# Softmax normalisation split between VectorE and GpSimd, and k rotated on GpSimd without a break

## The reference, cut to what matters

```
q = rope(layernorm(x) @ wq.T)      16 heads of 64
k = rope(ctx @ wk.T)
v = ctx @ wv.T
scores = where((j <= i) & (j >= i - 64), q.k / 8, -1e30)
probs  = softmax(scores)           <- exp, row sum, multiply by 1/sum
x = x + tanh(g0) * ((probs @ v) @ wo.T)
x = x + tanh(g1) * ffn(layernorm(x))   2 shared experts, 16 routed experts, top 4, exact gelu
```

## Time and profile before

| | |
|---|---|
| median of the runs | 564.47 us |
| profiled execution | 565.92 us, span 564.1 us |
| TensorE busy | 524.5 us, 93% |
| VectorE busy | 323.0 us, 57% |
| ScalarE busy | 308.1 us, 55% |
| GpSimd busy | 278.9 us, 49%, nearly all of it before 330 us |
| granted TensorE clock, mean | 0.985 |
| GpSimd divides (L415) | 64, 1040 ns each |
| GpSimd turns (L402) and joins (L410) | 29 of each, 2409 and 2377 ns |

### The profile page before, as it was taken

The page is one execution under the profiler, slowest core; times in us unless marked ns, Lnnn a source line. Parts: engine busy times, 40 slices in busy tenths (PEclk is TensorE's granted clock), DMA queues, the critical chain, the costliest instruction groups (busy, mean ns, idle before and its releaser), DMA issues.

```text
span 564.1 us, 13070 instructions
## 1 busy us (share of the span) xinstructions
PE 524.5 (93%) x4914; PEld 460.8 (82%) x4914; DVE 323.0 (57%) x1043; ACT 308.1 (55%) x864; POOL 278.9 (49%) x203
## 2 busy tenths in 40 slices
PE   8869799999999999999889789889989998999997
PEld 5557788888888888988778679779978997889996
DVE  2965567456865667666656735463645454554444
ACT  4255686566675656757466745753345334533332
POOL 2798988688787867888678515530010001000000
PEclk9989899999999999999999999999989998999999
DMA  6523312111031101111111155207200540045000
GB/s 238 181 55 95 91 38 90 35 34 34 3 109 34 35 2 34 35 35 43 32 34 52 41 191 203 76 1 232 107 2 0 154 185 1 1 137 202 1 1 37
DMA packets 20173, 41.02 MB, mean 73 GB/s; under 512 B 2896, under 2 KB 3152, under 8 KB 20112
## 3 DMA queue, kind: packets, MB, share of 16 engines
q1 hardware_dynamic: 20112, 40.20, 22.8%
HBM read 30.62 MB, written 2.23 MB: 58 GB/s over the span
## 4 chain that ended last, share of the span: by engine, by line
PE 64%; issue 20%; DVE 7%; POOL 4%; ACT 3%; DMA 1%; POOLq 0%; ACTq 0%
PE ring L807 42%; PE psO L1005 6%; PE psS L974 5%; PE psS L807 5%; PE psT L986 4%; POOL wl L423 1%; DVE arena L642 1%; DVE wl L712 1%; ACT xn L547 1%; POOL rstd L449 1%; DVE arena L645 1%; DMA craw<-in_ctx 1%; PE ring L902 1%; ACT sneg L489 1%; PE psT L947 1%
## 5 line engine op out<-in xcount | busy, mean ns | idle before, releaser
L807 PE MATMUL ring<-xTh,wh 128*128 128x512 f32 x272 | 111.7, 411 | 3.7 <-DVE xTl L613 2.1
L807 PE MATMUL ring<-xTh,wl 128*128 128x512 f32 x272 | 107.3, 394 | 0.0
L807 PE MATMUL ring<-xTl,wh 128*128 128x512 f32 x272 | 107.3, 394 | 0.0
L489 ACT ACTIVATE sneg<-ring 128x512 f32<-128x512 f32 x72 | 43.0, 597 | 103.5 <-PE ring L807 96.4
L691 DVE TENSOR_TENSOR prob<-sneg,arena 128x512 f32<-128x512 f32 x64 | 45.9, 717 | 83.1 <-ACT sneg L489 82.7
L402 POOL TENSOR_TENSOR arena<-arena,sin 128x1024 f32<-128x1024 f32 x29 | 69.9, 2409 | 30.0 <-DVE arena L642 30.0
L807 PE MATMUL ring<-wh,oTh 128*128 128x256 f32 x272 | 78.5, 289 | 3.9 <-DVE oTl L699 2.8
L807 PE MATMUL ring<-wl,oTh 128*128 128x256 f32 x272 | 76.8, 282 | 0.0
L807 PE MATMUL ring<-wh,oTl 128*128 128x256 f32 x272 | 76.7, 282 | 0.0
L415 POOL TENSOR_TENSOR prob<-prob,rinv 128x512 f32<-128x512 f32 x64 | 66.5, 1040 | 20.4 <-DVE rinv L772 19.2
L410 POOL TENSOR_TENSOR arena<-arena 128x1024 f32<-128x1024 f32 x29 | 68.9, 2377 | 1.2
(11 more groups left out here) (118 smaller groups left out, 1194.1 us busy)
## 6 DMA issues: line engine op xcount, KB each, us to landing
arena<-gate_scratch SPq DMA_DIRECT2D x64, 256.0 KB, 6.6
raw<-in_e SPq DMA_DIRECT2D x18, 256.0 KB, 2.6
raw<-in_w SPq DMA_DIRECT2D x16, 256.0 KB, 3.6
arena<-arena SPq DMA_DIRECT2D x16, 256.0 KB, 3.1
arena<-arena SPq DMA_DIRECT2D x16, 192.0 KB, 3.4
craw<-in_ctx SPq DMA_DIRECT2D x4, 512.0 KB, 4.2
x<-in_x SPq DMA_DIRECT2D x4, 512.0 KB, 4.9
out<-x SPq DMA_DIRECT2D x8, 256.0 KB, 2.8
```

What stands on the lines that cost most here:

```text
L489: act.activation(act_g[:, n % 2, :], ring[0][:, n % 2, :], ACT.Gelu).then_inc(f_gelu, 1)
L807: last = pe.matmul(out, a, b, start=start and i == 0 and j == 0, stop=stop and i == n - 1 and j == 2, skip_group_check=check)
```

## The change

VectorE does the multiplication for the even chunks right behind its reciprocal, with a wait on its own instruction between the two. GpSimd does it for the odd chunks alone. The semaphore is split in two, one for each engine, and TensorE and VectorE wait for the one that belongs to the chunk. On GpSimd join(k) moves from step 3 up to step 2, right behind turn(k) and ahead of the divide of that step.

```diff
+        def normed(c):
+            return s_norm[c % 2], c // 2 + 1
...
             def divide(c):
-                pool.wait_ge(s_inv, c + 1)
+                pool.wait_ge(s_inv, c // 2 + 1)
                 pool.tensor_tensor(prob[:, c % BUFS, :, :], prob[:, c % BUFS, :, :],
                                    rinv[:, c % BUFS, :].unsqueeze(2).to_broadcast([P, TT, P]),
-                                   ALU.mult).then_inc(s_norm, 1)
+                                   ALU.mult).then_inc(s_norm[1], 1)
...
                     if k == 2 and u:
                         turn(1, u + 1)
-                    if k == 3 and u:
                         join(1, u + 1)
-                if 1 <= c <= CHUNKS:
+                if 1 <= c <= CHUNKS and c % 2 == 0:
                     divide(c - 1)
...
                 if c >= BUFS:
-                    dve.wait_ge(s_norm, c - BUFS + 1)
-                dve.reciprocal(rinv[:, c % BUFS, :], rsum[:, c % BUFS, :]).then_inc(s_inv, 1)
+                    dve.wait_ge(*normed(c - BUFS))
+                ins = dve.reciprocal(rinv[:, c % BUFS, :], rsum[:, c % BUFS, :])
+                if c % 2:
+                    ins.then_inc(s_inv, 1)
+                else:
+                    link(ins)
+                    dve.tensor_tensor(prob[:, c % BUFS, :, :], prob[:, c % BUFS, :, :],
+                                      rinv[:, c % BUFS, :].unsqueeze(2).to_broadcast([P, TT, P]),
+                                      ALU.mult).then_inc(s_norm[0], 1)
...
             def transpose_probs(c):
-                pe.wait_ge(s_norm, c + 1)
+                pe.wait_ge(*normed(c))
```

More of the change, by code:

```diff
@@ L152, in build @@
         s_pe, s_max, s_exp = sem("s_pe"), sem("s_max"), sem("s_exp")
-        s_inv, s_norm = sem("s_inv"), sem("s_norm")
+        s_inv = sem("s_inv")
+        s_norm = [sem("s_norm_v"), sem("s_norm_p")]
         p_pe, p_out = sem("p_pe"), sem("p_out")
```

## The result

The change makes the kernel **slower by 0.9%**: ratio 1.0087, 95% interval 1.0050 to 1.0124; medians 570.32 us against 567.04 us over 16 runs each. The means are 570.9 and 566.0 us when two long runs of the kernel before (1010.11 and 570.25 us) are left out, and the loss of about 4.9 us is their difference; the medians alone differ by 3.3 us. A second series gave 1.0086 (1.0054 to 1.0117). Forecast was 566.4 us, within 560 to 571, and a loss of 1.9 us. The direction and the class within 2% were right, the size was not.

The account below looks back on a forecast made before the run. TensorE sets the time, bound by the end of GpSimd's join(k) in ten units; +3.2 +2.0 -2.1 -1.2 -1.4 +1.4 = +1.9 us on the profiled 565.92 gives 567.8, less 1.45 for the run median: 566.4 us, range 560 to 571.

Parts of the forecast that it names:

- rival C: VectorE's multiplication is not blocked by GpSimd, one input being a 128x4 tile read repeatedly; -10.0, 554.5 us, chance 0.13.
- Rival B: GpSimd's divide(4u+1) gets in ahead of VectorE's waiting multiplication and ends 0.40 us earlier; -2.1, 562.4 us, chance 0.17.
- a typical unit: Attention unit where join(k) was the bound: divide(4u+1) ends at 122.24, so scores come 0.36 us later than before.
- the nine units: The seven units with 0.69 us of TensorE idle time plus units 12 and 14: 9 x 0.36 = +3.2 us.
- the cover of `oTl`: In a typical unit, `oTl` ends 1.07 us later, at 118.40; the y product wants it at 118.57, leaving 0.17 us.
- Unit 13: LayerNorm statistics on VectorE come 1.07 us later and one 0.40 push is added; scores at 293.33, not 291.30: +2.0 us.
- unit 1: Two weight remainders (2.5 us) ahead of join(k) now come behind it; scores at 63.64: -2.1 us.
- the start: The q product at 47.09 waits for the fourth weight remainder; two divides go (-2.0), two pushes come (+0.8): -1.2 us.
- the clock drop that goes: The granted clock of 0.76 for six microseconds, after TensorE's idle 3.13 us in unit 1, should go: -1.4 us.
- units 6 and 10: Two attention units for which the prediction's sum held no term.
- The clock near the end: A new clock dip in unit 13, where TensorE will idle 1.7 and then 2.7 us: +1.4 us, other bound 0.
- Rival D: 0.9 us idle ahead of the transposes drops the clock in the nine units; +12.6 on top, 579.0 us, chance 0.07.

Follow-up runs that it names:

- one_input: The change with VectorE's multiplication cut into four one-tensor-input instructions that also write an unread row sum, against the kernel before: ratio 0.9885, 560.23 us.

## Why the prediction was right or wrong

**Right: the blocking.** Waiting for the GpSimd instruction that runs, a push of what follows, VectorE going first when both want in: all three as read from L712, L782 and L442. The section "VectorE Performance Modes" of the Trainium skill's "Advanced Engine Details and Errata" names 2-port instructions only, and rival C stood for a multiplication free of GpSimd; the trace shows a two-input `tensor_tensor` taking 1.1 to 1.8 us longer than its 0.69 us. Rival B (GpSimd first) fell too: the divide stands directly behind join(k) and still took 1.49 us.

**Right: a typical unit.** +0.36 forecast, +0.33 measured. The pushes were 0.34 and 0.45 us, I took 0.40 for both. For the nine units that is +2.9 (without the clock's part in unit 14), forecast +3.2.

One reading inside it was wrong and cost nothing. I took 118.57 from the chain as the start of the y product, and so 0.17 us as the cover of `oTl`. The timeline before has the y product at 118.33, 1.00 us after `oTl` ends:

```profile
118.33 0.36 PE L807 MATMUL ring<-wh,oTh 128*128 128x256 f32 x1
```

In the changed kernel it starts 0.15 us after `oTl` ends, in units 1 to 14 but for 2, 6 and 10, and this is the sign that the prediction named for too little cover:

```profile
116.63 0.66 DVE L787 TENSOR_TENSOR oTl<-psO,oTh 128x512 fp32r<-128x512 f32 x1
...
117.43 0.36 PE L818 MATMUL ring<-wh,oTh 128*128 128x256 f32 x1
```

It makes the y product 0.20 us late in a typical unit and 1.1 us late in unit 12. That costs nothing, because divide(4u+1) ends later still; it is why TensorE idles 0.66 us in front of the transposes and not the 0.9 us forecast. The count "ten units" bound by join(k) was eleven, by the prediction's own list.

**Unit 13 right, unit 1 partly by luck.** Unit 13: +2.0 and +1.97, with the y product waiting 1.66 us and the transposes 2.67 us, as forecast. Unit 1: -2.1 and -2.0, but this stretch also holds the 0.67 us at 47.09 that I had counted under the start, and it took 20.01, 20.82 and 19.72 us in the three traces, as the clock fell for longer or shorter in it. Start and unit 1 together gave -2.3 us, against -3.3 forecast.

**Wrong: the clock drop that goes, -1.4.** This is the step that failed most. Unit 2 was to be 1.4 us shorter, it is 0.06 longer. The drop behind the 3.13 us did go (the granted clock is 1.00 through unit 2 in all three changed traces), but the next thing was late:

```profile
67.58 0.47 PE L818 MATMUL ring<-xTh,wh 128*128 128x512 f32 x1 [0.94 <-POOL wl L428]
```

The q product waits 0.94 us for the third of four weight remainders in a row. I had counted the 2.5 us that two of them no longer take ahead of join(k) as won in unit 1, and did not ask who waits for what stands behind them. Another 0.35 us or so is the lateness of units 6 and 10, below; some 0.2 us I have not followed.

**Wrong: the start, -1.2.** Unit 0 gives -0.28. I followed the weight remainder ahead of the q product at 47.09, but it no longer decides; what does are the transposes of chunk 1 ahead of it in TensorE's queue, and their divide. Ahead of that divide only one other divide is gone (-1.0 us), while join(q) is pushed (2.69 instead of 2.35 us) and so is the divide itself (1.49 us). In the three traces unit 0 took 15.87, 16.29 and 15.65 us.

```profile
43.42 0.89 PE L997 MATMUL psT<-ident,prob 128*128 128x128 f32 x4 [3.38 <-POOL prob L420]
```

**Wrong: units 6 and 10 at nothing.** They cost 0.35 us each. Their transposes do not wait for the divide. The chain of waits in unit 6 shows what they wait for:

```profile
151.21 1.21 DVE arena L649
...
153.59 1.34 ACT prob L560 x7
154.94 0.92 ACT arena L535
155.85 0.04 issue
155.90 3.12 PE ring L818 x24
```

VectorE's cosines are late behind the multiplication, so the maxima and ScalarE's exponentials are, and in ScalarE's queue the copy of v (L535) stands behind these. The y product needs the `ring` half that this copy frees. I had followed the lateness of VectorE to `oTl` only, not through ScalarE. Without the blocking (one_input) these two units take 18.56 us, as before.

**The clock near the end, +1.4.** Unit 14 and what follows lost 1.39 us in the mean, of which 0.27 is the schedule's in unit 14. In one of the three traces the clock fell behind unit 13's waits (0.79 from 292 to 300 us; unit 14: 21.34 instead of 19.88 us). In all three it fell at the very end of the stage, near 320 us; before, it fell there in one of three. So the term came out near its size (1.1 us), but by luck: in the place I gave it happened only once. Rival D, a drop in every typical unit, did not come.

In sum, measured less forecast: start and unit 1 +1.0, unit 2 +1.5, units 6 and 10 +0.7, the nine units and the clock near the end -0.6; 1.9 + 2.6 = 4.5 us.

## What to carry to other kernels

Before work is moved from GpSimd to VectorE, look in the trace for an instruction with the same operands that already runs beside GpSimd: its longest duration, not its shortest, is the price, and the engine that is relieved pays part of it back. Here a form with one SBUF tensor input and a row sum turned the same move from 0.9% slower into 1.15% faster; the same form without the row sum made it 5.9% slower. When something is put behind something else in a queue, ask for both who waits for it; and follow a late engine through each queue it feeds.

## What the runs showed of the hardware

A 128x128 multiplication by a per-partition scalar, with a row sum, took 0.34 us beside a busy GpSimd, and the next one started after 0.27 us. Without the row sum it took 0.28 us while GpSimd was idle, with the next after 0.20 us, but up to 2.42 us beside GpSimd and 0.87 us in the mean. The additional output makes the instruction a little longer and keeps it from waiting. The two-input multiplication blocks (1.8 and 2.5 us in a typical unit, 0.69 us alone) although its second input is only a 128x4 operand, read over and over. It also pushed the GpSimd instruction behind (join(q) 2.72 us); the plain multiplication waited as well but left the joins at 2.40 us in the mean. And each of the eleven gaps of TensorE ahead of scores that the profile before leaves at "issue" ended 0.10 us after a GpSimd join.
